# Attention in one kernel of two layers: half the transposes of six units by DMA moves and 32x32 block transposes on VectorE

## The chip, the core and the metric

The kernel runs on one NeuronCore of one Trainium2 chip. The metric is the device time of one execution in microseconds (us). TensorE is called PE, VectorE DVE, ScalarE ACT, GpSimd POOL, and SyncE, which issues every DMA of this kernel, SP.

## What is computed

Eight images of 512 channels by 1024 positions go through two layers, all in fp32. Cut to what matters:

```python
# layer 0
hn = group_norm(x)
q, k, v = split(w_qkv @ hn + b_qkv)          # 8 heads of 64 channels
wgt = softmax(scale * q.T @ k, axis=-1)      # per head 1024 x 1024
a = v @ wgt.T
x = x + group_norm(w_proj @ a + b_proj)
# layer 1
qkv = w_qkv1 @ x ; qkv = qkv / rms(qkv)      # one head of 512 channels
x = (x + w_out1 @ (softmax(q.T @ k * s) @ v)) * 2**-0.5
```

In layer 0 the softmax matrix comes out with the queries on the partitions and the keys along the free dimension. The product with v needs the keys on the partitions, so the whole matrix has to be transposed.

## The kernel before, in words

**Split products.** To keep fp32 accuracy at the matmul rate of the reduced type, each operand is kept as a hi part (a rounded copy, made by ACT) and a lo part (the operand minus its hi part, made by DVE or POOL), and a product is the sum of two or three matmuls.

**Units and steps.** Per image (batch `b`), layer 0 has 16 units. Unit `u` is one head and one half of the queries; four units make a pair of heads. A unit has four steps `tb`, one for each block of 128 queries, and eight slots `s`, one for each block of 128 keys, numbered `n = 8*u + s`. A step counter runs from 0 to 68. In step `step`:

- PE first computes, in steps 5, 7, 9 and 11 of every 16 except the last 16, a q or k projection of the next pair (12 matmuls; line 468, `project_qk`); then the scores of the step's query block (4 matmuls, line 595, `scores0`) into one of two `big` buffers in PSUM; then the transposes of slots n and n+1 with n = 2*(step-5) (8 transposes, line 568, into `tps0` and `tps1` in PSUM); then the value products of slots n-2 and n-1 (4 matmuls, line 581, `values0`).
- DVE takes the lo part of the projection (line 1205, `qk_lo`), the negated row maximum of the scores (line 1213, `row_max`), the reciprocal of the previous block's row sum (line 1219, `recip`), and the lo parts of the two transposed slots (line 1224, `pt_lo`). In the first step of a unit `recip` comes before `row_max`, otherwise after it.
- ACT takes the hi part of the projection (line 841), the hi parts of the two transposed slots (line 855, `pt_hi`), a correction every other step, and the exponential of the scores into PB (line 849, `exps`).
- POOL multiplies the block in PB by its reciprocal row sum (line 989, `normalise`), sums a unit's output (line 999), makes some lo parts of the output (line 1014, `a_lo`), and scales the residual x (line 1008, `scale_x`) after steps 20, 23, 26 and 29.

Each engine works through its own list in program order and waits on counting semaphores. PE waits before the transposes of a unit for `s_p_norm`, before slot n's transposes for the lo part of slot n-2, and before the value product of slot n for the lo part of slot n. A `big` buffer is used again only after its last reader: the exponential for scores, `qk_lo` for a projection.

**Slots.** PT holds four slots of hi and lo parts; slot s of a unit uses place s % 4. PB holds eight query blocks, that is two units.

**The queue of DMAs.** SP is in order too: it waits, then issues. In layer 0 its list per image is: the weights of the second pair, the stacking of q and k of pair 0 (`stack_head`, line 384), the load of x into X (line 398), after the last value projection the weights of pairs 2 and 3 (line 402), then stackings of the later pairs with the loads of the output and Gram weights (lines 404 and 409) between them.

**Layer 1** turns its softmax matrix in another way already: 16 DMAs for each half (line 441) move blocks of 32 rows of PB to W0, from quarter to quarter of the partitions, and DVE block transposes of 32x32 (line 1386, `turn`) finish the transposition.

## Time and profile before

| | us |
|---|---|
| median of 3 runs | 3465.83 |
| lowest and highest | 3462.20, 3466.53 |
| the profiled execution's own time | 3466.39 |
| its span, from first to last instruction | 3464.6 |
| PE, DVE, ACT, POOL busy in the span | 3400.3, 2114.8, 1835.3, 1064.7 |
| mean granted PE clock, share of full speed | 0.996 |

The profile names an instruction by its line, its engine and its operands. A timeline row has the start in us from the span's start, the duration, the engine, the line, and how many instructions of the same kind it merges. Matmuls, and DVE and ACT instructions, overlap their neighbours a little, so the spacing of starts is less than the duration. The profiled execution is the run of 3466.39 us, 1.8 us longer than its span and 0.56 us above the median.

### The profile page before, as it was taken

To read this page: it belongs to the slowest core of one execution; us is meant where nothing else is said; L and a number is where in the kernel's file an instruction comes from. 1 tells how busy PE (TensorE), PEld (TensorE's weight loads), DVE (VectorE), ACT (ScalarE), POOL (GpSimd) and SP (SyncE) were. 2 spreads that over 40 slices of the span, in tenths; PEclk is the share of its full clock that TensorE was granted. 3 is DMA by queue.
4 is the path that set the end of the run, shared out by engine and by line. 5 is a ranking of instruction groups with operands and counts; after the bars stand their busy time and mean duration, and the time that the engine had idled before them with its cause. 6 is when DMAs were issued, how large, how long until landed. Compare 5 with 4: busy or idle time off the path is not lost.

```text
span 3464.6 us, 51840 instructions
## 1 busy us (share of the span) xinstructions
PE 3400.3 (98%) x16816; PEld 2776.6 (80%) x16816; DVE 2114.8 (61%) x3452; ACT 1835.3 (53%) x3082; POOL 1064.7 (31%) x947
## 2 busy tenths in 40 slices
PE   8999999999999999999999999999999999999999
PEld 4788878888788887887778877788777888788887
DVE  4577456773577735786457854578455784557744
ACT  3577226772278622785227842378323882247822
POOL 0244213442034410354104531145211452114511
PEclk9999999999999999999999999999999999999999
DMA  8512235212443125341153312442224422343212
GB/s 314 159 40 62 92 111 146 55 57 84 132 120 90 33 92 145 88 98 72 45 171 80 80 74 66 149 98 62 92 58 137 98 62 92 83 140 70 61 55 73
DMA packets 109849, 332.10 MB, mean 96 GB/s; under 512 B 21744, under 2 KB 54768, under 8 KB 98800
## 3 DMA queue, kind: packets, MB, share of 16 engines
q1 hardware_dynamic: 109552, 328.45, 33.3%
q8 instruction: 149, 2.44, 0.3%
q14 instruction: 148, 1.21, 0.1%
HBM read 162.68 MB, written 31.49 MB: 56 GB/s over the span
## 4 chain that ended last, share of the span: by engine, by line
PE 87%; DVE 4%; DMA 3%; ACT 2%; issue 2%; SPq 1%; POOL 0%; ACTq 0%; DVEq 0%; POOLq 0%
PE big L468 24%; PE big L595 13%; PE ops L581 13%; PE tps L568 13%; PE ops L734 10%; PE big L665 7%; PE big L633 5%; PE ops L468 3%; DMA ST<-ST 1%; SPq L384 1%; DMA d_m<-PT 1%; ACT PB L849 1%; DVE X L1369 1%; DMA d_u<-ST 1%; ACT PB L938 0%
## 5 line engine op out<-in xcount | busy, mean ns | idle before, releaser
L989 POOL TENSOR_SCALAR PB<-PB,small 128x1024 f32<-128x1024 f32 x576 | 651.8, 1132 | 1325.4 <-DVE small L1219 1314.6
L1213 DVE TENSOR_REDUCE small<-big 128x1 f32<-128x1024 f32 x512 | 625.0, 1221 | 100.9 <-PE big L595 97.6
L1224 DVE TENSOR_TENSOR PT<-tps,PT 128x512 fp32r<-128x512 f32 x1024 | 651.8, 678 | 32.4 <-ACT PT L855 32.0
L855 ACT ACTIVATE PT<-tps 128x512 fp32r<-128x512 f32 x1024 | 566.3, 597 | 147.6 <-PE tps L568 144.9
L849 ACT ACTIVATE PB<-big,small 128x1024 f32<-128x1024 f32 x512 | 572.1, 1117 | 100.6 <-DVE small L1213 97.6
L581 PE MATMUL ops<-PT,VT 128*128 128x512 f32 x2048 | 599.1, 414 | 0.0
L595 PE MATMUL big<-ST 128*128 128x512 f32 x2048 | 555.0, 393 | 10.2 <-DMA ST<-ST 10.2
L568 PEld LDWEIGHTS tps<-ident,PB 128*128 128x128 f32 x4096 | 467.4, 140 | 116.2 <-DVE PT L1224 55.9
L568 PE MATMUL tps<-ident,PB 128*128 128x128 f32 x4096 | 551.4, 275 | 8.9 <-DVE PT L1224 6.1
L595 PEld LDWEIGHTS big<-ST 128*128 128x128 f32 x2048 | 383.1, 188 | 98.4 <-issue 12.6
L581 PEld LDWEIGHTS ops<-PT,VT 128*128 128x128 f32 x2048 | 346.1, 189 | 47.2 <-DVE PT L1224 5.0
L468 PE MATMUL big<-HH,W 128*128 128x512 f32 x1024 | 333.7, 390 | 1.5 <-DVE ST L1087 1.1
L1205 DVE SCALAR_TENSOR_TENSOR ST<-big,vec,ST 128x512 fp32r<-128x512 f32 x128 | 96.1, 751 | 326.3 <-ACT ST L841 326.3
L841 ACT ACTIVATE ST<-big,vec 128x512 fp32r<-128x512 f32 x128 | 88.2, 689 | 299.8 <-PE big L468 299.8
L468 PEld LDWEIGHTS big<-HH,W 128*128 128x128 f32 x1024 | 192.3, 188 | 45.4 <-issue 4.2
L734 PE MATMUL ops<-PT,VT 128*128 128x512 f32 x768 | 196.2, 406 | 20.7 <-DVE PT L1392 16.7
L999 POOL TENSOR_TENSOR XA<-RB 64x512 f32<-64x512 f32 x128 | 163.8, 1280 | 142.7 <-ACT RB L866 141.5
L938 ACT ACTIVATE PB<-PB,small 128x1024 f32<-128x1024 f32 x56 | 69.7, 1245 | 252.1 <-POOL small L1052 252.1
L468 PE MATMUL big<-HL,W 128*128 128x512 f32 x512 | 199.8, 390 | 0.0
L734 PEld LDWEIGHTS ops<-PT,VT 128*128 128x128 f32 x768 | 145.7, 194 | 67.2 <-DVE PT L1392 20.6
L1052 POOL TENSOR_SCALAR small<-small 128x1 f32<-128x1 f32 x64 | 16.9, 263 | 553.9 <-DVE small L1357 540.6
L665 PE MATMUL big<-ST,W 128*128 128x512 f32 x720 | 182.6, 394 | 1.2 <-ACT XA L907 1.2
(151 smaller groups left out, 4803.9 us busy)
## 6 DMA issues: line engine op xcount, KB each, us to landing
ST<-ST SPq DMA_DIRECT2D x384, 256.0 KB, 5.0
W<-d_qk SPq DMA_DIRECT2D x32, 1024.0 KB, 6.3
W<-PB SPq DMA_DIRECT2D x256, 128.0 KB, 2.4
XA<-in_x SPq DMA_DIRECT2D x8, 2048.0 KB, 7.6
X<-in_x SPq DMA_DIRECT2D x8, 2048.0 KB, 10.6
W<-d_wp SPq DMA_DIRECT2D x8, 2048.0 KB, 11.9
W<-d_g SPq DMA_DIRECT2D x8, 2048.0 KB, 12.3
W<-d_m SPq DMA_DIRECT2D x8, 2048.0 KB, 7.8
```

The costliest lines, as they stand in the source:

```text
L468: last = mm(dst, stat(sp_, k), mov(mp_, k), start=(i == 0), stop=(i == n - 1))
L568: last = nc.tensor.transpose(tps[n % 2][:, P * t:P * t + P], PB[:, 4 * (u % 2) + t, P * s:P * s + P], ident[:])
L581: last = mm(ops[u % 2][:], VT[:, s, P * (u // 2):P * (u // 2) + P], pt_slot(u, s)[:, part, :], start=(s == 0 and part == 0), stop=(s == 7 ...
L595: last = mm(t[:, cols], stack("q", head)[:, tok:tok + P], stack(kind, head)[:, cols], start=(i == 0), stop=(i == 1))
L633: last = mm(t[:, cols], w_full[1][:, wp, k, P * o:P * o + P], (HH, HL)[ap][:, k, cols], start=(k == 0 and i == 0), stop=(k == PAIRS - 1 an ...
L665: last = mm(t[:, cols], w_full[slot][:, wp, j, P * k:P * k + P], x1(xp, j)[:, cols], start=(j == 0 and i == 0), stop=(j == (k if slot == 0 ...
L734: last = mm(ops[use % 2][:], VT[:, s, col:col + P], ptb[:, pp, :], start=(s == 0 and i == 0), stop=(s == 7 and i == 2))
L849: act_fn(PB[:, i, :], t[:], ACT.Exp, bias=negmax[:, i:i + 1], accum_out=rowsum[:, i:i + 1])\
L855: act_fn(pt_slot(u, s)[:, 0, :], tps[n % 2][:], ACT.Copy).then_inc(s_pt_hi, 1)
L989: nc.gpsimd.tensor_scalar(PB[:, i, :], PB[:, i, :], rinv[:, i:i + 1], 1.0, ALU.mult, ALU.mult)\
L1213: V.tensor_reduce(negmax[:, i:i + 1], tile(("s", 4 * u + tb))[:], axis=AX.X, op=ALU.max, negate=True).then_inc(s_row_max, 1)
L1224: V.tensor_tensor(pt_slot(u, s)[:, 1, :], tps[n % 2][:], pt_slot(u, s)[:, 0, :].bitcast(f32), ALU.subtract).then_inc(s_pt_ready, 1)
```

## The change

In units 0, 1, 4, 5, 8 and 9 of each image (`MOVED`) the slots s = 4 to 7 (`MOVED_SLOTS`, 24 of 128 per image) are no longer transposed by PE.

- The exponential of these units writes its row with every four adjacent elements taken from four different key blocks, so its writes step by 4 fp32 elements (16 bytes). PE's transposes of slots 0 to 3 read PB with the same step.
- When all four blocks of the unit are normalised, SP issues 16 DMAs (`move_quarters`), each of 32 partitions by 4 rows of 512 bytes, from PB into F0, the first half of X.
- DVE makes four block transposes (`square`) from F0, reading with a step of 4 elements, into the second half of X: slots n+2 and n+3 at the end of a step.
- The hi parts of these slots (ACT) and the lo parts read X in SBUF in place of PSUM. The lo parts of the odd slots (12 per image, `POOL_LO`) move from DVE to POOL, each after that step's `normalise`, in the list of POOL (`pool_lo`).
- ACT waits for `s_slot_free`, which PE raises after a value product, before it fills a place of PT with a moved slot.
- X now serves for the exchange, so the load of x is issued after slot 79's lo part, behind the first stacking of the last pair and before the Gram weights, and `scale_x` runs after steps 50, 52, 54 and 56.

```diff
+MOVED = moved_units(PAIRS - 1)        # 0, 1, 4, 5, 8, 9
+MOVED_SLOTS = [8 * u + s for u in MOVED for s in range(4, NT)]
+POOL_LO = [n for n in MOVED_SLOTS if n % 2]
-X_SCALE_STEPS = (20, 23, 26, 29)
+X_SCALE_STEPS = (50, 52, 54, 56)
...
+        F0 = X[:, 0:2, :].rearrange("p a (b n) -> p (a b) n", n=HALF).rearrange("p q (t n) -> p q t n", t=KB)
+        def squared(s):
+            return X[:, 2 + (s - 4) // 2, HALF * (s % 2):HALF * (s % 2) + HALF]
...
+                def move_quarters(u):
+                    half = u % 2
+                    sp.wait_ge(s_p_norm, b * 72 + 4 * u + 4)
+                    own_wait(sp)
+                    if u:
+                        sp.wait_ge(s_squared, squared_count(b, 8 * MOVED[MOVED.index(u) - 1] + NT - 1))
+                    own_wait(sp)
+                    for tq in range(QUARTERS):
+                        for sq in range(QUARTERS):
+                            sp.dma_start(F0[32 * sq:32 * sq + 32, tq, :, :],
+                                         PB[32 * tq:32 * tq + 32, 4 * half:4 * half + 4,
+                                            HALF + P * sq:HALF + P * sq + P]).then_inc(s_moved[half], 16)
+
                 sp.wait_ge(s_out_done, (b * 8 + CREDIT) * 16)
                 own_wait(sp)
-                sp.dma_start(X[:], src_x(b)).then_inc(s_x_res, 16)
                 sp.wait_ge(s_v_full, b * 4 + 4)
                 own_wait(sp)
+                move_quarters(0)
                 for i in (2, 3):
                     sp.dma_start(w_qk(i).rearrange("p h k n -> p (h k n)").bitcast(f32), d_qk[i]).then_inc(ld_qk[i], 16)
+                move_quarters(1)
                 stack_head(b, 1, 0)
                 sp.dma_start(W[1][:].bitcast(f32), d_wp[:]).then_inc(s_ld_wp, 16)
                 stack_head(b, 1, 1)
+                move_quarters(4)
+                move_quarters(5)
                 stack_head(b, 2, 0)
                 stack_head(b, 2, 1)
+                move_quarters(8)
+                move_quarters(9)
                 stack_head(b, 3, 0)
+                sp.wait_ge(s_pt_ready, lo_count(b, 79))
+                own_wait(sp)
+                sp.wait_ge(s_pool_lo, pool_lo_count(b, 79))
+                own_wait(sp)
+                sp.dma_start(X[:], src_x(b)).then_inc(s_x_res, 16)
                 sp.dma_start(W[0][:].bitcast(f32), d_g[:]).then_inc(s_ld_g, 16)
...
@@ transposes (PE)
+                        if u in MOVED:
+                            keys = row[:, 0:HALF].rearrange("p (k s) -> p s k", s=4)[:, s, :]
@@ values0 (PE)
-                    pe.wait_ge(s_pt_ready, b * 144 + n + 1)
+                    if n in POOL_LO:
+                        pe.wait_ge(s_pool_lo, pool_lo_count(b, n))
+                    else:
+                        pe.wait_ge(s_pt_ready, lo_count(b, n))
@@ PE's list
-                        transposes(n // 8, n % 8)
-                        transposes(n // 8, n % 8 + 1)
+                        for m in (n, n + 1):
+                            if m not in MOVED_SLOTS:
+                                transposes(m // 8, m % 8)
@@ exps (ACT)
+                    if u in MOVED:
+                        to = to.rearrange("p (h q r s) -> p h s q r", h=2, q=QUARTERS, s=4)
+                        scores = scores.rearrange("p (h s q r) -> p h s q r", h=2, q=QUARTERS, s=4)
@@ POOL's list
+                def pool_lo(n):
+                    u, s = n // 8, n % 8
+                    pool.wait_ge(s_pt_hi, b * 144 + n + 1)
+                    own_wait(pool)
+                    nc.gpsimd.tensor_tensor(pt_slot(u, s)[:, 1, :], squared(s), pt_slot(u, s)[:, 0, :].bitcast(f32),
+                                            ALU.subtract).then_inc(s_pool_lo, 1)
                 for n in range(4 * UNITS0):
                     normalise(n)
+                    if 2 * (n + 1 - LAG) + 1 in POOL_LO:
+                        pool_lo(2 * (n + 1 - LAG) + 1)
@@ DVE
+                def square(n):
+                    u, s = n // 8, n % 8
+                    if n in POOL_LO and POOL_LO.index(n) > 1:
+                        dve.wait_ge(s_pool_lo, pool_lo_count(b, n) - 2)
+                    if s == 4:
+                        dve.wait_ge(s_moved[u % 2], moved_count(b, u))
+                    V.transpose(squared(s).rearrange("p (t q r) -> p t q r", t=KB, q=QUARTERS),
+                                F0.rearrange("p q t (r s) -> p s t q r", s=4)[:, s - 4, :, :, :])\
+                     .then_inc(s_squared, 1)
...
                         pt_lo(n // 8, n % 8)
-                        pt_lo(n // 8, n % 8 + 1)
+                        if n + 1 not in POOL_LO:
+                            pt_lo(n // 8, n % 8 + 1)
+                    for m in (n + 2, n + 3):
+                        if m in MOVED_SLOTS:
+                            square(m)
```

## Rows read from the trace of the kernel before

**Rows 1.** The page: busy time and share per engine, and the chain that ended last.

```profile
PE 3400.3 (98%) x16816; PEld 2776.6 (80%) x16816; DVE 2114.8 (61%) x3452; ACT 1835.3 (53%) x3082; POOL 1064.7 (31%) x947
...
PE 87%; DVE 4%; DMA 3%; ACT 2%; issue 2%; SPq 1%; POOL 0%; ACTq 0%; DVEq 0%; POOLq 0%
```

**Rows 2.** Timeline of PE, steps 7 and 8 of the second image (start us, us, engine).

```profile
555.63 1.07 PE L595 MATMUL big<-ST 128*128 128x512 f32 x4
556.54 1.03 PE L568 MATMUL tps<-ident,PB 128*128 128x128 f32 x8
557.33 1.17 PE L581 MATMUL ops<-PT,VT 128*128 128x512 f32 x4
558.33 1.07 PE L595 MATMUL big<-ST 128*128 128x512 f32 x4
559.25 1.15 PE L568 MATMUL tps<-ident,PB 128*128 128x128 f32 x8
560.15 1.17 PE L581 MATMUL ops<-PT,VT 128*128 128x512 f32 x4
561.16 0.39 PE L468 MATMUL big<-HH,W 128*128 128x512 f32 x1
```

**Rows 3.** Timeline of DVE in the same image, steps 7 and 11.

```profile
556.55 0.75 DVE L1205 SCALAR_TENSOR_TENSOR ST<-big,vec,ST 128x512 fp32r<-128x512 f32 x1 [2.76 <-ACT ST L841]
...
558.42 1.27 DVE L1224 TENSOR_TENSOR PT<-tps,PT 128x512 fp32r<-128x512 f32 x2
...
573.10 0.75 DVE L1205 SCALAR_TENSOR_TENSOR ST<-big,vec,ST 128x512 fp32r<-128x512 f32 x1 [2.74 <-ACT ST L841]
```

**Rows 4.** Timeline of POOL: blocks 2 and 3, then 6, then 7.

```profile
543.16 2.21 POOL L989 TENSOR_SCALAR PB<-PB,small 128x1024 f32<-128x1024 f32 x2 [2.50 <-DVE small L1219]
...
558.70 1.13 POOL L989 TENSOR_SCALAR PB<-PB,small 128x1024 f32<-128x1024 f32 x1 [4.77 <-DVE small L1219]
560.07 1.12 POOL L989 TENSOR_SCALAR PB<-PB,small 128x1024 f32<-128x1024 f32 x1 [0.24 <-DVE small L1219]
```

**Rows 5.** Groups of instructions by line (count, busy us, mean ns, idle before).

```profile
L1014 POOL TENSOR_TENSOR HL<-XA,HH 128x512 fp32r<-128x512 f32 x48 | 61.8, 1287 | 3.8 <-POOL XA L999 3.8
...
L568 PEld LDWEIGHTS tps<-ident,PB 128*128 128x128 f32 x4096 | 467.4, 140 | 116.2 <-DVE PT L1224 55.9 <-POOL PB L989 1.0
```

**Rows 6.** Timeline of SP at the first exchange DMAs of layer 1, and their landing.

```profile
888.05 0.60 SPq L441 DMA_DIRECT2D W<-PB  x1
...
888.70 1.27 SPq L441 DMA_DIRECT2D W<-PB  x2
...
DMA to landing us min/median/max: 2.3/2.4/3.8
```

**Rows 7.** Timeline of DVE: six block transposes of layer 1.

```profile
877.67 3.67 DVE L1386 STREAM_TRANSPOSE PB<-W 128x512 f32<-128x512 f32 x6
```

**Rows 8.** Pair 1 of the same image: block 19 on POOL, step 23 on DVE.

```profile
598.24 1.14 POOL L989 TENSOR_SCALAR PB<-PB,small 128x1024 f32<-128x1024 f32 x1 [0.48 <-DVE small L1219]
...
611.52 0.75 DVE L1205 SCALAR_TENSOR_TENSOR ST<-big,vec,ST 128x512 fp32r<-128x512 f32 x1 [2.76 <-ACT ST L841]
```

**Rows 9.** Layer 1: POOL, and a DVE lo part with two SBUF inputs, side by side.

```profile
886.26 1.68 POOL L989 TENSOR_SCALAR PB<-PB,small 128x1024 f32<-128x1024 f32 x1
...
886.87 1.61 DVE L1392 TENSOR_TENSOR ST<-PB,ST 128x512 fp32r<-128x512 f32 x1
```

**Rows 10.** The page's DMA issues: the load of x.

```profile
X<-in_x SPq DMA_DIRECT2D x8, 2048.0 KB, 10.6
```

**Rows 11.** An idle PE in the first image: its row, and a stretch with its clock (0.50).

```profile
104.14 2.07 PE L595 MATMUL big<-ST 128*128 128x512 f32 x4 [6.69 <-DMA ST<-ST]
...
102.00:104.00 2.00, 0.00 (x0) 0.00 (x0) 0.00 (x0) 0.00 (x0) 0.00 (x0) 0.50 1.04 227
```

More of the change, by code:

```diff
@@ L46, in qk_part, with moved_units @@
     return None
+def moved_units(pairs):
+    return [u for pair in range(pairs) for u in (4 * pair, 4 * pair + 1)]
+MOVED = moved_units(PAIRS - 1)
+MOVED_SLOTS = [8 * u + s for u in MOVED for s in range(4, NT)]
+POOL_LO = [n for n in MOVED_SLOTS if n % 2]
 def a_parts(step):
@@ L163, in turned, with t_count, lo_count, pool_lo_count @@
             return PB[:, 4 * c + s // 2, HALF * (s % 2):HALF * (s % 2) + HALF]
+        F0 = X[:, 0:2, :].rearrange("p a (b n) -> p (a b) n", n=HALF).rearrange("p q (t n) -> p q t n", t=KB)
+        def squared(s):
+            return X[:, 2 + (s - 4) // 2, HALF * (s % 2):HALF * (s % 2) + HALF]
+        def t_count(b, n):
+            return b * (8 * UNITS0 - len(MOVED_SLOTS)) + len([m for m in range(n + 1) if m not in MOVED_SLOTS])
+        def lo_count(b, n):
+            return b * (8 * UNITS - len(POOL_LO)) + n + 1 - len([m for m in POOL_LO if m <= n])
+        def pool_lo_count(b, n):
+            return b * len(POOL_LO) + POOL_LO.index(n) + 1
+        def squared_count(b, n):
+            return b * len(MOVED_SLOTS) + MOVED_SLOTS.index(n) + 1
+        def moved_count(b, u):
+            i = MOVED.index(u)
+            return (b * (len(MOVED) // 2) + i // 2 + 1) * EXCHANGE
         def by_quarter(row):
@@ L228, in build @@
         s_pt_ready = sem("pt_ready")
+        s_moved = [sem("moved_even"), sem("moved_odd")]
+        s_squared = sem("squared")
+        s_slot_free = sem("slot_free")
+        s_pool_lo = sem("pool_lo")
         s_o_full = sem("o_full")
@@ L565, in transposes @@
                     if n >= 2:
-                        pe.wait_ge(s_pt_ready, b * 144 + n - 1)
+                        pe.wait_ge(s_pt_ready, lo_count(b, n - 2))
                     for t in range(4):
-                        last = nc.tensor.transpose(tps[n % 2][:, P * t:P * t + P],
-                                                   PB[:, 4 * (u % 2) + t, P * s:P * s + P], ident[:])
+                        row = PB[:, 4 * (u % 2) + t, :]
+                        if u in MOVED:
+                            keys = row[:, 0:HALF].rearrange("p (k s) -> p s k", s=4)[:, s, :]
+                        else:
+                            keys = row[:, P * s:P * s + P]
+                        last = nc.tensor.transpose(tps[n % 2][:, P * t:P * t + P], keys, ident[:])
                     last.then_inc(s_t_full, 1)
@@ L584, in values0 @@
                         last.then_inc(s_o_full, 1)
+                    elif n + 4 in MOVED_SLOTS:
+                        last.then_inc(s_slot_free, 1)
                 def scores0(u, tb):
@@ L729, in values1 @@
                     if e < 2:
-                        pe.wait_ge(s_pt_ready, b * 144 + 8 * (UNITS0 + c) + s + 1)
+                        pe.wait_ge(s_pt_ready, lo_count(b, 8 * (UNITS0 + c) + s))
                     ptb = pt_slot(UNITS0 + c, s)
@@ L848, in exps @@
                     i = 4 * (u % 2) + tb
-                    act_fn(PB[:, i, :], t[:], ACT.Exp, bias=negmax[:, i:i + 1], accum_out=rowsum[:, i:i + 1])\
+                    to, scores = PB[:, i, :], t[:]
+                    if u in MOVED:
+                        to = to.rearrange("p (h q r s) -> p h s q r", h=2, q=QUARTERS, s=4)
+                        scores = scores.rearrange("p (h s q r) -> p h s q r", h=2, q=QUARTERS, s=4)
+                    act_fn(to, scores, ACT.Exp, bias=negmax[:, i:i + 1], accum_out=rowsum[:, i:i + 1])\
                         .then_inc(s_exp_done, 1)
@@ L853, in pt_hi @@
                     n = 8 * u + s
-                    act.wait_ge(s_t_full, b * 128 + n + 1)
-                    act_fn(pt_slot(u, s)[:, 0, :], tps[n % 2][:], ACT.Copy).then_inc(s_pt_hi, 1)
+                    if n in MOVED_SLOTS:
+                        act.wait_ge(s_squared, squared_count(b, n))
+                        act.wait_ge(s_slot_free, squared_count(b, n))
+                        turned0 = squared(s)
+                    else:
+                        act.wait_ge(s_t_full, t_count(b, n))
+                        turned0 = tps[n % 2][:]
+                    act_fn(pt_slot(u, s)[:, 0, :], turned0, ACT.Copy).then_inc(s_pt_hi, 1)
                 def corr(u, part):
@@ L1015, in a_lo @@
                                             ALU.subtract).then_inc(s_a_lo, 1)
+                def pool_lo(n):
[4 more added lines that the diff above has]
+                                            ALU.subtract).then_inc(s_pool_lo, 1)
+                    pool.wait_ge(s_pool_lo, pool_lo_count(b, n))
+                    own_wait(pool)
                 for n in range(4 * UNITS0):
                     normalise(n)
+                    if 2 * (n + 1 - LAG) + 1 in POOL_LO:
+                        pool_lo(2 * (n + 1 - LAG) + 1)
                     if n % 4 == 3 and n >= 8:
```

4 lines of the change are left out of this document (3 added, 1 removed).

## The prediction, made before any run of the changed kernel

> **What bounds the kernel now.** I read the page first: PE is busy 98% of the span and the chain that ended last is PE for 87% [rows 1]. So work taken off PE counts at once, as long as nothing that replaces it is late. Next the timeline of two steps, because the change acts inside a step [rows 2]. The reader is to see how tightly PE's list is packed: scores at 555.63, transposes at 556.54, values at 557.33, scores of step 8 at 558.33, transposes at 559.25, values at 560.15, projection at 561.16. Start to start, eight transposes cost 0.79 us in step 7 and 0.90 us in step 8. I then read what DVE and POOL do in these steps [rows 3, 4], since they make what PE waits for, and last the one exchange by DMA that the kernel has, in layer 1 [rows 6].
>
> I count from the scores of step 7 (555.63 = 0). PE's projection of step 9 then starts at 5.53; DVE's `qk_lo` starts at 0.92 and its pair of `pt_lo` at 2.79; POOL normalises block 6 from 3.07 and block 7 from 4.44 to 5.56.
>
> **What is taken away.** Per unit, 16 transposes in two steps: 0.79 + 0.90 = 1.69 us. There are 6 units x 8 images = 48, so at most 81 us. That is the whole gain: 3466.4 - 81 = 3385 if all that replaces it were on time.
>
> **The handoff inside step 8.** In unit 0 the moved slots 4 and 5 are due in step 8. Without transposes PE goes scores (0.91), values 2 and 3 (1.00), scores of step 8 (0.92), and stands before the value product of slot 4 at 2.83. Its lo part is DVE's at 2.79 + 0.68 = 3.47 (half of the pair's 1.27 plus overlap), since `row_max` and `recip` of this step come first as before. The product of slot 4 takes 0.5, to 3.97. Slot 5 hangs on POOL, whose list has `normalise(6)` ahead of `pool_lo(5)`: 3.07 + 1.09 (half of the two blocks' 2.21, less the overlap) + 1.29 for the lo part, by the nearest row, a POOL subtraction of the same size [rows 5] = 5.45. Its product ends at 5.95, where the step ended at 5.53 before. So PE waits 1.5 us for POOL and the 1.69 us are spent: the unit ends 0.42 later than it did. To this comes that `pt_lo(4)` now has two SBUF inputs. In layer 1 such an instruction and `normalise` held each other up: 1.68 us where it takes 1.13, and 1.61 where DVE's takes 0.65 [rows 9]. Here `normalise(6)` would start at 3.07 in the middle of `pt_lo(4)`, which ends at 3.47. I add 0.40 (bounds 0 and 0.96, DVE's whole extra), so the handoff costs **0.8 us per unit**. The ACT copies of moved slots (SBUF in place of PSUM) hang on squares made a step ahead and lie beside `row_max`: nothing.
>
> **The exchange.** The 16 DMAs have the shape of layer 1's, 32 partitions by 4 rows, with rows half as long. The first of those, on an idle queue, kept SP for 0.60 us, and the next started 0.65 later [rows 6]. So the issue itself takes that long, not the data, and I take it for the new ones too: 15 x 0.65 + 2.4 to land = **12.15 us**. Bounds: no less than 15 x 0.33 + 2.3 = 7.2, if half the bytes took half the time; no more than 9.75 + 3.8 = 13.5, by the longest landing.
>
> Squares 4 and 5 come at the end of step 6 on DVE. DVE is then idle until `qk_lo` of step 7, for 2.76 us [rows 3]. Two squares take 2 x 0.61 = 1.2 (six took 3.67) [rows 7], so they cost nothing if the exchange has landed by 0.92 - 1.2 = -0.28. Block 3 is normalised at 543.16 + 2.21 = 545.37 [rows 4], which is -10.26. The exchange lands at +1.89: **2.17 us late**. DVE waits with its whole list behind it: `qk_lo` (PE's scores of step 8 need its buffer), `row_max(7)`, `recip(6)`, and through POOL the value product of slot 5. The lateness passes to PE in full.
>
> In pairs 1 and 2 the last block is done at 598.24 + 1.14 = 599.38 and `qk_lo` of the moved step comes at 611.52 [rows 8]: landing at 611.53 against 610.32, **1.21 us late**.
>
> For the second unit of a pair the exchange starts with block 7. POOL now has `pool_lo(5)` before it, so it ends at 3.07 + 1.09 + 0.40 + 1.29 + 1.13 = 7.0 plus the first lateness, not at 5.56. Landing is then 19.15 plus that lateness. The limit is `qk_lo` of step 11, 573.10 [rows 3], less 1.2: 16.27, moved by the first lateness and by 0.8. The difference is **2.08 us late**, in any pair. Squares 6 and 7 take DVE time (1.2 us) that the two lo parts given to POOL (1.2 us) leave free: nothing.
>
> **Other edits.** The load of x moves behind slot 79, about step 45; it takes 10.6 us to land [rows 10] and is wanted after block 50. It shares the engines with the Gram weights and delays the last stacking, which is due only in step 56. I cost both at nothing; cover gone, the image would wait some us for the stacking, once. `scale_x` runs where POOL has `a_lo` too: per step 1.1 + 1.3 or 1.1 + 1.05, below a step of 2.7. SP's waits for `s_p_norm` stand ahead of the weights of pairs 2 and 3 and of the stackings, all due steps later: nothing. The `s_slot_free` wait asks for products of the step before, long done.
>
> **The steps of 4 elements** (exponential's writes, PE's reads of slots 0 to 3, the squares' reads) are shown by no row; nothing in the trace has such a step. A gain has no cause. Below: no cost. Above: each access doubled, a square 0.61 more and a transpose's weight load 0.28 in place of 0.14 [rows 5]. I take nothing, as no row shows a strided access slower, and carry the doubling as a rival.
>
> The Trainium skill, page "Advanced Engine Details and Errata", section "SBUF Cachelines", speaks against this layout: SBUF has 16-byte lines, and accesses that each fall in another line are slower. No row of this case shows it. [...]
>
> **The sum.** Pair 0: 2.17 + 0.8 + 2.08 + 0.8 = 5.85. Pairs 1 and 2: 1.21 + 0.8 + 2.08 + 0.8 = 4.89 each. An image: 15.63; eight: 125 us. On the profiled execution's 3466.4 that is 3591.4; the median is 0.6 lower, so **3591 us**. This case's own range: without the contention 3572; with landings of 3.8 us 3658; with issues 0.60 apart and landings of 2.3, 3550.
>
> **Rivals.**
>
> 1. *The exchange is on time, the handoff stays.* If shorter rows are issued in 0.33 us, the exchange takes 7 us and no unit is late. What is left is 0.42 to 0.8 x 48 = 20 to 38 us: 3487 to 3505. Against it: the first issue took 0.60 on an empty queue. 9%.
> 2. *Strided access is slow.* Squares alone: two of them stand before `qk_lo`, +1.22 x 48 = 59, 3650. With PE's loads, which then set the spacing (16 x (0.28 - 0.11) = 2.7 per unit), another 130: 3780. No row shows it, and none excludes it. The Trainium skill's rule named above is for it. 13%.
> 3. *PE's clock falls.* PE idle for 6.69 us came back at 0.50 and its four score matmuls took 2.07 us [rows 11]. Here its waits are 1 to 2 us each, with matmuls between. If it fell once per unit, a projection and a scores group at half speed would cost 3.6 us more: 3765. 5%.
> 4. *Faster: both handoffs in time.* If the exchange takes under 10 us and `pool_lo(5)` ends by 3.97, PE is held by `pt_lo(4)` alone: products from 3.47 to 4.48, against 5.53, saves 1.05 x 48 = 50: 3416. It decides at the moment when PE reaches slot 5. For: DVE has the idle time for the squares. Against: POOL's list puts 1.1 us of normalising before it, from 3.07 on. 12%.
> 5. *The two cancel*, within 0.2% (7 us, about what a measurement of this kernel can tell from no change): an exchange in time and half of POOL's wait gone. 3%.
>
> The forecast itself has 58%. **Chances**: faster 0.12, same 0.03, slower 0.58 + 0.09 + 0.13 + 0.05 = 0.85. **Range**: 3480 to 3700 takes in the forecast, rival 1 and the squares' part of rival 2; it leaves out rival 4, the cancelling, and the far ends of 2 and 3, about 2 in 10.
>
> **What the new profile would show.** Right: the idle time of DVE before line 1205 falls, and a new wait of DVE for the exchange stands there, 1.2 to 2.2 us before slot 4 or 12, 48 times (about 90 us in all); PE waits at line 581 for POOL, some 1 to 1.5 us, 48 times; SP's new issues last 0.60; the transposes fall from 4096 to 3328. PE's busy share falls to about 92%. Wrong: issues of 0.33; a DVE that never waits for the moves; squares of over 0.8 us or exponentials of two lengths (then rival 2); a clock of 0.5 in the attention stretches; or a step 8 that ends before 5.5 us after the scores of step 7.

## The result, and the profile after

The changed kernel takes **3720.78 us** (median of 4 runs, 3719.81 to 3723.12) against 3466.18 us for the kernel before in the same comparison (4 runs): ratio 1.0737, 95% interval 1.0719 to 1.0756, 255 us more. The forecast was 3591, its range ended at 3700. The direction was right, and the loss was twice the one forecast. The profiled execution took 3719.81 us, its span is 3717.8 us, its mean granted PE clock 0.972 against 0.996 before.

The page of the changed kernel: busy time, the chain that ended last by engine, then groups (count, busy us, mean ns, idle time before them and its releaser) and the new DMAs (KB each, us to landing).

```profile
PE 3451.1 (93%) x16048; PEld 2742.9 (74%) x16048; DVE 2276.8 (61%) x3548; ACT 1998.0 (54%) x3082; POOL 1218.0 (33%) x1043
...
PE 55%; SPq 13%; DVE 9%; issue 8%; ACT 6%; DMA 5%; POOL 3%; DVEq 0%; ACTq 0%; POOLq 0%
...
L927 ACT ACTIVATE PB<-big,small 128x1024 f32<-128x1024 f32 x512 | 764.6, 1493 | 123.5 <-DVE small L1308 120.6
...
L1329 DVE STREAM_TRANSPOSE X<-X 128x512 f32<-128x512 f32 x192 | 200.7, 1087 | 160.6 <-DMA X<-PB 160.6
...
X<-PB SPq DMA_DIRECT2D x768, 64.0 KB, 2.0
```

Against [rows 1], PE has 768 instructions fewer and is busy 51 us **longer**; SP, which issues the moves, is now 13% of the chain. Line 927 is the exponential and line 1329 the square. What waited for what, in us in total, times, and the longest:

```profile
DVE X L1329 <- DMA X<-PB: 160.6, 48, 4.7
ACT PT L939 <- DVE X L1329: 121.6, 137, 3.0
PEld big L668 <- DVE ST L1300: 119.9, 45, 4.0
...
PEld ops L652 <- POOL PT L1105: 87.6, 48, 1.9
```

The first wait is the late exchange, in all 48 units. The second is ACT, whose copies of the moved slots wait for the squares. The third is what the late exchange does to PE: its scores stand for `qk_lo` (line 1300). The fourth is the handoff to POOL (line 1105 is `pool_lo`, 652 the value product); it is counted on PE's loads of weights, and PE's matmuls themselves waited 58.8 us there. Now the step of [rows 2], the same one of the second image, as a timeline of the changed kernel:

```profile
589.10 1.09 PE L668 MATMUL big<-ST 128*128 128x512 f32 x4
...
591.30 2.06 DVE L1329 STREAM_TRANSPOSE X<-X 128x512 f32<-128x512 f32 x2 [3.61 <-DMA X<-PB]
...
593.27 0.72 DVE L1300 SCALAR_TENSOR_TENSOR ST<-big,vec,ST 128x512 fp32r<-128x512 f32 x1
...
594.04 1.71 PE L668 MATMUL big<-ST 128*128 128x512 f32 x4 [2.94 <-DVE ST L1300]
...
595.15 2.15 ACT L927 ACTIVATE PB<-big,small 128x1024 f32<-128x1024 f32 x1 [1.14 <-DVE small L1308]
...
595.68 2.13 DVE L1329 STREAM_TRANSPOSE X<-X 128x512 f32<-128x512 f32 x2
...
598.07 1.22 PE L652 MATMUL ops<-PT,VT 128*128 128x512 f32 x2 [1.01 <-POOL PT L1105]
...
599.09 0.63 PE L532 MATMUL big<-HH,W 128*128 128x512 f32 x1
...
602.90 1.08 PE L668 MATMUL big<-ST 128*128 128x512 f32 x4
```

Three things are to be seen. DVE idles 3.61 us for the moves; two squares then take 2.06 us in place of the 1.2 expected; and from the scores of step 8 on PE runs slowly: four score matmuls 1.71 us instead of 1.07, a projection matmul 0.63 instead of 0.39. From the scores of step 7 to those of step 9 it is 13.80 us, where it was 563.91 - 555.63 = 8.28 before. The windows of 10 us (the column behind the five engines is the granted clock) show when the clock fell:

```profile
580.00:590.00 10.00, 9.30 (x47) 7.34 (x46) 5.78 (x9) 8.31 (x12) 2.25 (x2) 1.00 0.40 94
590.00:600.00 10.00, 5.95 (x16) 3.44 (x15) 8.70 (x11) 5.51 (x7) 4.25 (x4) 0.73 0.61 221
600.00:610.00 10.00, 10.00 (x50) 8.47 (x49) 5.56 (x10) 5.85 (x11) 3.41 (x3) 0.93 0.39 92
```

So three causes stood to be priced: steps of 4 elements, exchange, clock. My theory after this result (S in the expectations): the steps of 4 elements are what the forecast left out, and without them the time comes back near it. The rivals: the steps cost little because they lie beside other work, and the late exchange with the fallen clock costs the whole 255 us; POOL's lo parts, not the exchange, hold PE; the later load of x adds something.

### The profile page after: what moved, and what is told of

Its sections match the earlier page's. It is cut to its first block, busy times and chain, and to the rows that moved or that the text cites. A ratio compares the mean times of both kernels' runs of the same rounds, so it can differ in the third digit from the quotient of the medians.

```text
span 3717.8 us, 51900 instructions
## 1 busy us (share of the span) xinstructions
PE 3451.1 (93%) x16048; PEld 2742.9 (74%) x16048; DVE 2276.8 (61%) x3548; ACT 1998.0 (54%) x3082; POOL 1218.0 (33%) x1043
## 4 chain that ended last, share of the span: by engine, by line
PE 55%; SPq 13%; DVE 9%; issue 8%; ACT 6%; DMA 5%; POOL 3%; DVEq 0%; ACTq 0%; POOLq 0%
PE big L532 15%; SPq L446 12%; PE ops L808 9%; PE big L739 6%; PE big L668 6%; PE tps L637 6%; PE ops L652 6%; PE big L707 5%; ACT PB L927 3%; DMA X<-PB 3%; DVE small L1308 2%; POOL PB L1073 2%; DVE X L1329 2%; PE ops L532 2%; ACT PT L939 1%
## 5 line engine op out<-in xcount | busy, mean ns | idle before, releaser
L1073 POOL TENSOR_SCALAR PB<-PB,small 128x1024 f32<-128x1024 f32 x576 | 664.5, 1154 | 1449.7 <-DVE small L1314 1415.4
L927 ACT ACTIVATE PB<-big,small 128x1024 f32<-128x1024 f32 x512 | 764.6, 1493 | 123.5 <-DVE small L1308 120.6
L668 PE MATMUL big<-ST 128*128 128x512 f32 x2048 | 594.3, 414 | 137.2 <-DVE ST L1300 107.9
L652 PE MATMUL ops<-PT,VT 128*128 128x512 f32 x2048 | 633.1, 428 | 73.9 <-POOL PT L1105 58.8
L1320 DVE TENSOR_TENSOR PT<-tps,PT 128x512 fp32r<-128x512 f32 x832 | 532.5, 681 | 53.2 <-ACT PT L939 52.9
L939 ACT ACTIVATE PT<-tps 128x512 fp32r<-128x512 f32 x832 | 455.9, 598 | 132.0 <-PE tps L637 130.7
L652 PEld LDWEIGHTS ops<-PT,VT 128*128 128x128 f32 x2048 | 358.9, 197 | 172.2 <-POOL PT L1105 87.6
L637 PEld LDWEIGHTS tps<-ident,PB 128*128 128x128 f32 x3328 | 403.5, 158 | 105.8 <-DVE PT L1320 65.8
L637 PE MATMUL tps<-ident,PB 128*128 128x128 f32 x3328 | 467.6, 282 | 9.7 <-DVE PT L1320 6.7
L532 PE MATMUL big<-HH,W 128*128 128x512 f32 x1024 | 346.3, 404 | 1.5 <-DVE ST L1182 1.1
L1329 DVE STREAM_TRANSPOSE X<-X 128x512 f32<-128x512 f32 x192 | 200.7, 1087 | 160.6 <-DMA X<-PB 160.6
L808 PE MATMUL ops<-PT,VT 128*128 128x512 f32 x768 | 195.3, 405 | 21.7 <-DVE PT L1502 17.7
```

What stands on the lines that cost most here:

```text
L532: last = mm(dst, stat(sp_, k), mov(mp_, k), start=(i == 0), stop=(i == n - 1))
L637: last = nc.tensor.transpose(tps[n % 2][:, P * t:P * t + P], keys, ident[:])
L652: last = mm(ops[u % 2][:], VT[:, s, P * (u // 2):P * (u // 2) + P], pt_slot(u, s)[:, part, :], start=(s == 0 and part == 0), stop=(s == 7 ...
L668: last = mm(t[:, cols], stack("q", head)[:, tok:tok + P], stack(kind, head)[:, cols], start=(i == 0), stop=(i == 1))
L808: last = mm(ops[use % 2][:], VT[:, s, col:col + P], ptb[:, pp, :], start=(s == 0 and i == 0), stop=(s == 7 and i == 2))
L927: act_fn(to, scores, ACT.Exp, bias=negmax[:, i:i + 1], accum_out=rowsum[:, i:i + 1])\
```

## The experiments

Each was compared with runs of the kernel before beside it, whose medians were 3465.07, 3466.29, 3465.53, 3466.91 and 3465.57 us.

**1. No step of 4 elements (e1_blocks).** The order of the keys comes from the score product, which reads the second half of the keys in blocks of 32; exponential and transposes are plain, the squares read runs of 32.

```diff
@@ scores0 (PE)
+                            if u in MOVED and half:
+                                keys = keys.rearrange("p (s q r) -> p q s r", s=4, q=QUARTERS)
...
@@ exps (ACT)
-                        to = to.rearrange("p (h q r s) -> p h s q r", h=2, q=QUARTERS, s=4)
-                        scores = scores.rearrange("p (h s q r) -> p h s q r", h=2, q=QUARTERS, s=4)
...
@@ square (DVE)
-                                F0.rearrange("p q t (r s) -> p s t q r", s=4)[:, s - 4, :, :, :])
+                                F0.rearrange("p q t (s r) -> p s t q r", s=4)[:, s - 4, :, :, :])
```

> The changed kernel without any step of 4 elements: PE reads the second half of the keys in blocks of 32 in the score product, so the exponential writes a plain row, PE transposes plain columns, and the squares read runs of 32. Moves, waits, lo parts on GpSimd stay. Theory S (the steps of 4 elements are what the forecast left out, and the exchange and handoff cost what it said): exponentials 1.12 us, squares 0.70 us, and a time near the forecast, 3580 to 3610. Rival X (the steps lie beside other work; the late exchange with the fallen clock costs the whole 255 us): above 3680.

Measured: 3638.61 us, 1.0497 [1.0480, 1.0515], so **82 us of the 255 are the steps of 4**. That is neither range: theory S wanted 110 us or more from the steps, its rival at most 40. Groups and the wait for the moves in its profile:

```profile
L924 ACT ACTIVATE PB<-big,small 128x1024 f32<-128x1024 f32 x512 | 572.2, 1118 | 152.5 <-DVE small L1305 149.6
...
L1326 DVE STREAM_TRANSPOSE X<-X 128x512 f32<-128x512 f32 x192 | 124.9, 688 | 165.5 <-DMA X<-PB 165.5
...
DVE X L1326 <- DMA X<-PB: 165.5, 48, 5.4
```

The exponential is back at 1.12 us and the square at 0.69, and the wait for the exchange is as long as before. This is also the kernel that my sum described, so its timeline is the one to hold against it:

```profile
580.82 1.08 PE L668 MATMUL big<-ST 128*128 128x512 f32 x4
...
582.79 1.30 DVE L1326 STREAM_TRANSPOSE X<-X 128x512 f32<-128x512 f32 x2 [3.79 <-DMA X<-PB]
...
584.02 0.71 DVE L1297 SCALAR_TENSOR_TENSOR ST<-big,vec,ST 128x512 fp32r<-128x512 f32 x1
...
588.79 1.22 PE L649 MATMUL ops<-PT,VT 128*128 128x512 f32 x2 [1.00 <-POOL PT L1102]
...
589.81 0.63 PE L532 MATMUL big<-HH,W 128*128 128x512 f32 x1
...
593.92 1.09 PE L668 MATMUL big<-ST 128*128 128x512 f32 x4
```

**2. Plain exponential alone (e2_exp_plain)** takes the two lines of `exps` in that diff and leaves the rest of the change as it is; the keys then stand in another order than the moves and transposes take them.

> The changed kernel, but the exponential of the six units writes a plain row (the keys then stand in another order than the moves and transposes take them, so the product with v pairs wrong keys; the work is the same). Squares and PE's reads keep their step of 4. Theory S: ACT's share is the larger part, 3610 to 3640 (squares 0.4 us longer, twice before qk_lo, 48 times, are left: 38 us over e1). If the squares and PE's reads are the larger part: 3660 to 3700. Rival X: 3690 to 3720.

Measured: 3671.45 us (one run). The exponential is 49 us of the 82, the squares and PE's reads the other 33. The time falls into the range that stood for squares and PE's reads as the larger part, but that range hung on a lower time of e1_blocks; against the time that e1_blocks took, the exponential is the larger part.

**3. The steps alone (e8_stride_only)**: the kernel before, nothing moved, with the strided exponential in the six units and PE's transposes of all their slots reading with the step.

> The kernel before, with nothing moved: only the six units' exponentials write with a step of 4 elements, and PE transposes all their slots with reads of that step. Theory S: exponentials of 2.1 us make ACT (2.1 + 1.1 for two hi parts = 3.2 us a step) slower than PE's 2.7 us in the 24 steps per image, less where a projection stands in the step: 0.5 us x 16 steps x 8 = 60 us, and PE's reads 0.1 us per 8 (48 units x 4 groups) = 20 us: 3530 to 3550. If ACT's longer work is hidden: within 10 us of the kernel before, 3466.

Measured: 3514.58 us, 1.0143 [1.0126, 1.0160], again 49 us more, with the clock at 0.997: under the range of theory S, and far over its rival's. ACT's exponential, PE's loads of weights, and PE's wait for the exponential in its profile:

```profile
L856 ACT ACTIVATE PB<-big,small 128x1024 f32<-128x1024 f32 x512 | 765.8, 1496 | 71.0 <-DVE small L1220 67.6
...
L572 PEld LDWEIGHTS tps<-ident,PB 128*128 128x128 f32 x4096 | 505.6, 165 | 102.0 <-DVE PT L1231 56.2 <-POOL PB L996 0.9
...
PEld big L598 <- ACT PB L856: 41.8, 56, 1.1
```

The mean load went from 140 [rows 5] to 165 ns over 4096, which is (165 - 140) x 4096 / 1536 = 67 ns on each of the 1536 strided ones. This run does not part those loads from the exponential by itself, but the spacing of the 512 groups of score matmuls does. Against the kernel before, 43 of the 49 us fall on seven spacings per image (scores of steps 4 to 5, 18 to 21 and 34 to 37), which are the 56 waits above. In the changed kernel the same seven lose 43 us, and in e2_exp_plain, where PE's reads still step by 4, none. So about 43 us are the exponential; the rest of the 49 is spread over other steps, by about 0.1 us a step.

**4. A quarter of the moves (e4_four_moves)**: the change with 4 DMAs for each exchange instead of 16.

```diff
-                        for sq in range(QUARTERS):
+                        for sq in range(1):
```

> The changed kernel with 4 of the 16 moves per unit (the other twelve are left out, so three quarters of the moved slots are stale data; squares, waits and all else stay). An exchange takes about 3 x 0.65 + 2.0 = 4 us in place of 12. DVE's wait for it, 160.6 us in the changed kernel, should be gone. If a late exchange passes to the end one for one: 3720.8 - 160 = 3560, and up to 25 less if the clock stays up. If the chain through the longer exponential and the handoff holds the end anyway: above 3640.

Measured: 3585.99 us (one run), 135 us less than the change and 26 over what I expected if the lateness passed on one for one; its clock is 0.988 against 0.972. A quarter of the moves is also less traffic on the queue; PE's waits for the stackings of q and k stay what they were (8 times, 9.9 us here and 9.8 in the change).

**5. Both at once (e5_blocks_four)**: e1_blocks with 4 moves.

> e1 (no step of 4 elements) with 4 of the 16 moves per unit, so that no exchange is late (three quarters of the moved slots are stale data). What is left of the change is the handoff: PE's transposes gone, the odd lo parts on GpSimd behind the normalising. Theory S, as the prediction had it: 0.42 to 0.8 us per unit over the kernel before, 3486 to 3505. If a clock that falls at PE's waits adds to it: up to 3560. If the transposes taken away are worth something once all is on time: below 3460.

Measured: 3544.11 us, 1.0228 [1.0211, 1.0245], in the range that stood for a clock that falls too. Against e1_blocks **the exchange on time is worth 94.5 us**, and the clock went from 0.978 to 0.987. With neither steps nor lateness the kernel still loses 78 us, where my sum had 38 (0.8 a unit) left. Its timeline of PE shows why, in two first units of the second image, that of pair 0 and that of pair 2:

```profile
571.56 0.73 PE L649 MATMUL ops<-PT,VT 128*128 128x512 f32 x2 [1.49 <-POOL PT L1102]
...
572.13 0.39 PE L532 MATMUL big<-HH,W 128*128 128x512 f32 x1
...
574.87 1.07 PE L668 MATMUL big<-ST 128*128 128x512 f32 x4
...
685.49 0.88 PE L649 MATMUL ops<-PT,VT 128*128 128x512 f32 x2 [1.49 <-POOL PT L1102]
686.16 0.63 PE L532 MATMUL big<-HH,W 128*128 128x512 f32 x1
...
690.39 0.84 PE L668 MATMUL big<-ST 128*128 128x512 f32 x3
```

Both wait 1.49 us for POOL. In the first the scores of steps 7 and 9 (565.82 and 574.87) are 9.05 apart, 0.77 more than before: the 0.8 of my sum. In the other (679.75 and 690.39) they are 10.64 apart, because the projection runs at half the rate for most of its length, 4.23 us instead of 2.74. Same waits, another clock: the granted clock is 0.62 over that projection and 1.00 over the first, and the difference is 1.5 us a time. Over all eight images the scores of steps 8 and 9 are 7.2 us apart with the clock at 1.00 in ten of the 24 first units, and 8.6 to 8.8 us with the clock at 0.80 or 0.81 in the other fourteen. First units lose 41 us in all, 22 of them by this, and second units 27 us.

**6. All lo parts on DVE (e6_blocks_four_dve)**: e5_blocks_four with an empty `POOL_LO`.

> e5 with all lo parts on VectorE. The value product of slot 5 then waits for DVE's second lo part (about 4.1 us after the scores of step 7) in place of GpSimd's (about 5.5 to 7). First unit: 0.3 us gained on the kernel before, since the exponential of step 8 then comes last; second unit: 0.4 lost, as no projection follows to cover DVE. So within 10 us of the kernel before, 3456 to 3476. The rival that GpSimd's handoff is no term of the sum: within 5 us of e5.

Measured: 3530.29 us, 1.0184 [1.0167, 1.0201]: 14 us less than e5_blocks_four, and outside both ranges. In the first unit of pair 0 (second image) the scores of steps 7 and 9 are now at 564.31 and 572.05, 7.74 apart: under the 8.28 of the kernel before, and 1.3 under the 9.05 with POOL. But in its second unit those of steps 11 and 14 are at 580.31 and 590.66, 10.35 apart, where it was 592.58 - 583.15 = 9.43 with POOL and 8.26 before. The timeline shows what took the gain back, at the first transposes of the next unit:

```profile
587.56 0.42 PEld L632 LDWEIGHTS tps<-ident,PB 128*128 128x128 f32 x4 [1.91 <-DVE PT L1315]
...
589.23 0.42 PEld L632 LDWEIGHTS tps<-ident,PB 128*128 128x128 f32 x4 [1.26 <-DVE PT L1315]
```

PE's transposes still wait for the lo part of slot n-2, although an exchanged slot never used their buffer. With the lo part of slot 7 on DVE too, that wait became the last one; no projection follows here to hide it. DVE's two lo parts took 2.50 us there, beside work of POOL, and 1.27 in the step before. Over all images the first units save 9 us and the second lose 71.

**7. x later (e7_x_late)**: the kernel before with only the load of x and `scale_x` moved.

> The kernel before with one part of the change: the load of x behind slot 79, and its scaling after steps 50, 52, 54 and 56. Prediction: nothing, within 5 us of 3465. If the stacking of the last pair or the residual waits for it: 1 to 8 us per image, 3475 to 3530.

Measured: 3465.57 us, 0.9998 [0.9988, 1.0007]. Nothing, as forecast.

**8. PE's work put back (e9_ghost_transposes)**: e1_blocks, in which PE also does the 768 transposes, of the identity, which nobody reads; its waits are those of the buffers alone.

```diff
@@ transposes (PE)
+                        if n in MOVED_SLOTS:
+                            keys = ident[:]
...
@@ PE's list
-                            if m not in MOVED_SLOTS:
-                                transposes(m // 8, m % 8)
+                            transposes(m // 8, m % 8)
```

> e1 with PE's 768 transposes put back, of the identity matrix and read by nobody: the same waits as e1, but PE has the 81 us of work again, inside the steps where it waits. If PE's saved work is worth nothing, because others set the steps: within 10 us of e1's 3638.6. If the fallen clock is a real part of e1's time, more work in the gaps keeps it up, and the time is lower than e1's, 3590 to 3630. If the saved work counts: above 3690.

Measured: 3623.70 us, 1.0452 [1.0434, 1.0469]: with 768 more transposes it is **15 us faster** than e1_blocks, and the clock of the profiled execution is 0.992 instead of 0.978. So where a unit is late, the transposes saved are worth nothing, and the gaps that they leave cost more than the work did. The waits of the transposes for lo parts, the one other thing that was changed, come to the same in both profiles (PE's loads at that line waited 46.8 us in e1_blocks and 47.7 here), and DVE's wait for the moves is not shorter (185.8 against 165.5 us). So the clock is the reason that is left, and the timelines show it. The scores of steps 8 and 9, with the projection between them, in the 24 first units of each profile:

| | us apart | granted clock |
|---|---|---|
| e1_blocks, 14 units | 7.2 to 7.3 | 1.00, in one unit 0.77 |
| e1_blocks, 10 units | 8.7 to 9.3 | 0.62 to 0.81 |
| e9_ghost_transposes, 24 units | 7.2 to 7.4 | 1.00 |

In all, first units lose 79 us in e1_blocks and 56 in e9_ghost_transposes, which is what my sum had for them. Second units lose 89 and 101: where the first unit is not slowed, the second exchange has less time (in pair 0 of e1_blocks, first units that lose 4.8 to 5.0 us are followed by second ones that lose 1.2 to 3.1, and those that lose 3.2 and 3.0 by 6.6 and 4.6).

**9. Smaller and later (e11_late_split).** What would be left of the change if it kept to its means? Only the first unit of each of the first three pairs, only the last two slots, 16 moves of rows of 256 bytes; the squares one step later, behind `row_max`, and ACT's exponential of that step ahead of its two copies; runs of 32 instead of steps of 4.

```diff
@@ moved_units
-    return [u for pair in range(pairs) for u in (4 * pair, 4 * pair + 1)]
+    return [4 * pair for pair in range(pairs)]
...
-MOVED_SLOTS = [8 * u + s for u in MOVED for s in range(4, NT)]
+MOVED_SLOTS = [8 * u + s for u in MOVED for s in (6, 7)]
...
@@ DVE
+                    for m in (n, n + 1):
+                        if m in MOVED_SLOTS:
+                            square(m)
                     if n >= 0:
                         pt_lo(n // 8, n % 8)
```

> The change made smaller and given more time: only the first unit of each of the first three pairs is exchanged, and of it only the last two blocks of 128 keys (slots 6 and 7), with 16 moves of rows of 256 bytes. The score product puts the keys of the last quarter in order (two products of 256 columns for one of 512), the exponential and the squares read and write runs of 32. The squares run one step later than in the change, behind row_max, and ACT takes the exponential of that step ahead of the two copies. Theory A (the change lost only through late exchanges and steps of 4 elements; a saved transpose is worth its time once the exchange is on time): each of the 24 units saves PE the transposes of its last two slots, 0.90 us, so up to 22 us less than before, 3444 to 3455 after the short products are paid. Theory B (PE's saved time comes back as gaps at the handoff behind it, as putting the transposes back cost nothing): 3464 to 3480, with waits of values on the lo parts of slots 6 and 7. Theory C (even this exchange is late): over 3485, with DVE waiting for the moves by 1 us or more in each of the 24 units.

Measured: **3445.82 us**, 0.9946 [0.9933, 0.9960], 20 us less than before: it beats both kernels. Theory A held. The timeline, second image, scores of step 7 to scores of step 9:

```profile
548.57 1.07 PE L668 MATMUL big<-ST 128*128 128x512 f32 x4
...
551.28 1.08 PE L668 MATMUL big<-ST 128*128 128x512 f32 x4
...
553.89 1.29 DVE L1331 STREAM_TRANSPOSE X<-X 128x512 f32<-128x512 f32 x2
...
556.01 1.07 PE L668 MATMUL big<-ST 128*128 128x512 f32 x4
```

No wait for the moves, and 7.44 us instead of 8.28; 0.84 x 24 units = 20 us. The chain of squares, copy and lo parts runs while PE has its projection (548.57 + 2.71 to 556.01).

**10. What the order of keys costs there (e12_pieces_only)**: the kernel before, with the 256-column products of those units in plain order.

> The kernel before with the second half of the score products of units 0, 4 and 8 as two products of 256 columns instead of one of 512, in plain order, and nothing else. It prices what the run above pays for its order of keys. 192 more pairs of weight load and product in all. Theory A and B alike: 0 to 13 us more than before (3465 to 3479), nothing if a load of weights stays hidden behind a product of 256 columns.

Measured: 3468.25 us, 1.0009 [1.0000, 1.0018]: some 3 us, at the edge of what can be told from nothing.

**11. The second units as well (e13_late_both)**: `MOVED` back at six units, slots 6 and 7.

> The previous version (last quarter only, 16 moves of 256-byte rows, squares one step later) with the second unit of each of the first three pairs exchanged as well: 48 units instead of 24. The second unit has no projection of the next pair between its last normalise and its squares, and its last lo parts on GpSimd. Theory A (a saved transpose is worth its time where the exchange is on time): the first half gave 20 us for 24 units, so another 15 to 20 us if the second exchange is on time, 3425 to 3432. Rival (the second exchange is late): its 16 issues of 0.60 us and the 2.4 us of the last landing take 12.2 us from the last normalise; in the kernel before, the squares of a unit without a projection behind it would be wanted some 9 to 10 us after that point, so DVE waits 2 us or more in each of 24 units and the time is 3465 to 3500, with a wait of DVE on the moves of 48 us or more in all.

Measured: 3510.35 us, 1.0125 [1.0109, 1.0142]. The time is past even the rival's range, and **both theories were wrong on the cause**: no wait of DVE for the moves is in this profile. The timeline of the second unit's step 12 shows another wait:

```profile
576.18 1.09 PE L671 MATMUL big<-ST 128*128 128x512 f32 x4
...
576.82 1.29 DVE L1334 STREAM_TRANSPOSE X<-X 128x512 f32<-128x512 f32 x2
...
578.69 0.69 DVE L1325 TENSOR_TENSOR PT<-X,PT 128x512 fp32r<-128x512 f32 x1 [0.58 <-ACT PT L939]
...
579.43 0.68 PEld L635 LDWEIGHTS tps<-ident,PB 128*128 128x128 f32 x4 [2.60 <-DVE PT L1325]
579.44 0.87 PE L635 MATMUL tps<-ident,PB 128*128 128x128 f32 x3 [2.17 <-DVE PT L1325]
```

It is the wait of experiment 6: PE stands 2.60 us at the next unit's transposes for the lo part of slot 6. The clock falls behind it: between the scores at 576.18 and the next at 582.87 it is 0.75, and the eight transposes take 1.93 us instead of 1.03.

**12. That wait taken away (e14_late_both_free)**, and slot 7's lo part in the second units left on DVE.

```diff
@@ transposes (PE)
-                        pe.wait_ge(s_pt_ready, lo_count(b, n - 2))
+                        pe.wait_ge(s_pt_ready, lo_count(b, max(m for m in range(n - 1) if m % 2 == n % 2 and m not in MOVED_SLOTS)))
...
-POOL_LO = [n for n in MOVED_SLOTS if n % 2]
+POOL_LO = [n for n in MOVED_SLOTS if n % 2 and n // 8 % 2 == 0]
```

> The previous version with two edits. PE's transposes of slots n and n+1 no longer wait for the lo part of slot n-2 where that slot is exchanged (it never used their PSUM buffer), but for the last slot of the same parity that did; and in the second unit of a pair slot 7's lo part stays on DVE. The trace of the previous version shows DVE never waiting for the moves, and in the second unit, where no projection follows, PE idle for 2.6 us before the transposes of the next unit, released by the lo part of slot 6. Theory D (that wait between buffers, not the exchange, was what the second unit lost): the transposes come first, the lo parts end 1.3 us sooner than the one on GpSimd did, and the second units save something: 3425 to 3446, under the version that exchanges only the first units or level with it. Rival (without a projection behind the moved slots their chain of square, copy and lo part is too late for PE in any order): 3450 to 3490, with the wait moved from the transposes to the value product of slot 6.

Measured: 3479.17 us, 1.0042 [1.0028, 1.0055]. The rival held. 31 us came back, but most of it is the clock, and the wait only moved, to the value product:

```profile
580.64 1.30 DVE L1325 TENSOR_TENSOR PT<-X,PT 128x512 fp32r<-128x512 f32 x2 [0.58 <-ACT PT L939]
...
581.39 1.35 PE L650 MATMUL ops<-PT,VT 128*128 128x512 f32 x4 [1.21 <-DVE PT L1325]
```

The second unit's scores of steps 11 and 15 start at 573.46 and 585.80, 12.34 us apart, where before they were at 572.17 and 583.14, 10.97 apart: 1.37 x 24 = 33 us, which is the distance between this run and e11_late_split. The 24 second units, steps 11 to 15, tell where the 31 us came from. In e13_late_both nine of them lose 1.3 to 1.7 us and fifteen 2.8 to 3.3; here all lose 1.1 to 1.5. So at full clock the two edits are worth 0.2 us a unit, some 4 us in all, and some 24 us more are the slow clock behind the 2.6 us waits; the mean granted clock went from 0.991 to 0.997. The run does not part its two edits.

## Why the prediction was wrong in size

**The steps of 4 elements, "I take nothing": wrong, 82 us.** This is the step that failed most. The reason I gave, that no row shows a strided access slower, was the absence of a row, not a row that showed none. The exponential went from 1.12 to 2.1 us, the square from 0.69 to 1.09, a load of weights from 0.14 to about 0.21. The exponential, the largest term (49 us), was not priced at all, in rival 2 either: it priced the squares (59) and PE's loads (130) and missed the one instruction that nearly doubled. It is not hidden, because a score buffer is free only when the exponential has read it: PE's score loads waited 42.0 us, 56 times, for line 927 in the changed kernel, and 1.8 us for the plain one in e1_blocks. The Trainium skill, page "Advanced Engine Details and Errata", section "SBUF Cachelines", gives SBUF lines of 16 bytes and a penalty where each access falls in another line; it gives no size, and the doubling was my own bound. With that rule the trace agrees for ACT's writes (x1.9), for the squares' reads (x1.6) and for PE's loads (x1.5); I had the rule and gave it 13%.

**The exchange: right to a tenth in the first unit.** SP's issues lasted 0.601 us (median) and the last move landed 2.0 us later, where I had 0.60 and 2.4. In e1_blocks `qk_lo` starts 584.02 - 580.82 = 3.20 after the scores, against 0.92 in the kernel before: 2.28 late, forecast 2.17; in the first unit of pair 1 of that image it is 1.99, 1.07 late, forecast 1.21. In all, DVE waited 160.6 us, not the "about 90" that I wrote: the wait for the moves also contains idle time that DVE had there before (2.76 us, [rows 3]), which I had not counted in.

**The second unit: wrong in its places.** I had 2.08 + 0.8 in every pair. In the second image of e1_blocks the scores of steps 11 and 14 are 602.19 and 612.14, 9.95 apart against 580.43 - 572.17 = 8.26: 1.7 lost, as the half clock of the projection before had already made PE late. In pair 1 (steps 27 and 30) they are 660.68 and 675.28 against 627.14 and 635.68: 6.1 lost: there `qk_lo` came 4.22 after the scores, 3.3 late and not 2.08, and the clock fell again.

**The handoff, 0.8 a unit: right in its place and nearly in size.** PE waited for POOL in 48 places (87.6 us), as written. Where the exchange is on time and the clock is up (e5_blocks_four, second image) a first unit loses 0.77 and the second of pair 0 9.43 - 8.26 = 1.17. That `normalise` and the lo parts with two SBUF inputs hold each other up did show: in the changed kernel one such lo part took 1.16 us beside POOL, 0.69 otherwise. In e1_blocks POOL bore it: DVE's 96 such lo parts took 0.67 us on average, and `normalise` beside them 1.37 (586.13) instead of 1.12. The changed kernel:

```profile
595.09 0.69 DVE L1320 TENSOR_TENSOR PT<-X,PT 128x512 fp32r<-128x512 f32 x1
...
598.38 1.12 POOL L1073 TENSOR_SCALAR PB<-PB,small 128x1024 f32<-128x1024 f32 x1 [0.36 <-POOL PT L1105]
598.88 1.16 DVE L1320 TENSOR_TENSOR PT<-X,PT 128x512 fp32r<-128x512 f32 x1
```

**The clock, rival 3 at 5%: it came, on top of the forecast.** I wrote that PE's waits of 1 to 2 us have matmuls between them. They were up to 3.6 us, and in 590 to 600 us of the changed kernel PE was busy 5.95 us of 10 and its clock 0.73. In e1_blocks the first projection behind a moved slot takes 593.92 - 589.81 = 4.11 us instead of 2.75, part of it at 1.2 GHz and part at 2.4 (the granted clock is 0.50 from 588.79 to 591.80, and 0.79 from there to 593.92). That is 1.4 us in this unit, half of the 2.7 that rival 3 had for a projection. Even waits of 0.6 and 1.5 us in one step brought it down in some units (e5_blocks_four). Behind the first units' gaps alone it cost 18 us in e1_blocks (ten times, table above) and 22 in e5_blocks_four, and in e13_late_both some 24 us behind the second units'. It was not a case beside the forecast but a consequence of it, and belonged in its sum.

**The sum.** I forecast 125 us, 56 in first units and 69 in second ones, and e1_blocks, the kernel that it describes, lost 173: 79 in first units, 89 in second ones, and some 5 elsewhere. Of the 23 more in first units 18 are the clock between steps 8 and 9; with it up, e9_ghost_transposes loses 56 there. The 20 more in second units have the clock in them and an exchange that came later than forecast in pair 1. The steps add 82: 255. **x and `scale_x`: nothing**, as forecast. **The 81 us of saved transposes** did not appear at all where the exchange was late (e9_ghost_transposes) and appeared in full where it was on time and a projection stood behind it (e11_late_split, 0.84 of 0.90 us a unit).

What stays open: how the 20 us more in second units divide between the clock and the later exchange, and what wait or how many of them bring the clock down, as in e5_blocks_four the same two waits do it in one unit and not in another.

## What to carry to other kernels

Work taken off the bounding engine is worth its time only if the whole chain that replaces it ends before that engine comes by; look for the place with a cover (here a projection of 2.7 us) and move only what fits behind it. Price every access with a new step on every engine that makes it, by a run of that access alone if the trace has no such row. Where the bounding engine gets gaps, add its slower clock to them (here 1.5 us for each projection behind a gap in which it fell). Look for waits that guard a buffer which the changed step no longer uses.

## What was not expected of the hardware

- An ACT write of 128x1024 with a step of 16 bytes took 2.1 us against 1.12; a DVE block transpose of 128x512 that reads with this step 1.09 against 0.69 us; with runs of 128 bytes it took 0.69, as plain.
- The issue of a DMA of 32 partitions by 4 rows kept SP for 0.60 us with rows of 512 bytes (64 KB, [rows 6] had 128 KB), and in e11_late_split 16 issues of 32 KB still took the same: its 7 issues from 544.40 took 4.55 us. With this pattern the price did not change with the bytes.
- PE did 768 transposes more in less time (3623.70 against 3638.61 us), with the granted clock at 0.992 instead of 0.978; none of the 24 projections in first units ran slowly, where ten had.
